# The last chunk of a chunked state scan on three engines, and LayerNorm statistics in quarters

## What is computed

```python
xn = layernorm(x)
s = gated_linear_recurrence(rmsnorm(xn)) + xn        # layer 0, width 256
g = silu(top1_mixture_of_experts(xn))                # 4 experts, 256 -> 1024 -> 256
x = x + s * g
xn = layernorm(x)                                    # layer 1
# state space scan: 512 channels, 16 states n, time step l
xc = silu(causal_conv4(x_half)); delta = softplus(dt)
state[n] = exp(delta * A[n]) * state[n] + (delta * xc) * B[l, n]
y = sum over n of state[n] * C[l, n] + D * xc
s = (y * silu(z)) @ W_out.T + b_out
g = silu(xn @ binarized_W.T + bias)
x = x + s * g
```

## Time and profile before

| | |
|---|---|
| median of 3 runs | 1483.12 us (1483.07 to 6704.92) |
| profiled execution | 1484.12 us, of which its span is 1482.3 us |
| TensorE busy, share of the span | 95% |
| VectorE, ScalarE, GpSimd busy | 69%, 60%, 62% |
| last scan ends | 1452.93 us |
| last tile's store is issued | 1473.69 us |

### The profile page before, as it was taken

One profiled execution on the slowest core, in us unless ns is written; L12 is line 12 of the kernel. 1 busy time (PEld: TensorE's weight loads), 2 busy tenths in 40 slices (PEclk: granted clock), 3 DMA queues, 4 the chain that ended last, 5 costly groups with the idle time before them and its releaser, 6 DMA issues.

```text
span 1482.3 us, 24201 instructions
## 1 busy us (share of the span) xinstructions
PE 1405.9 (95%) x9104; PEld 1126.9 (76%) x9104; DVE 1025.2 (69%) x1348; ACT 887.0 (60%) x1457; POOL 926.4 (62%) x472
## 2 busy tenths in 40 slices
PE   4999999999999999779899999999999999999996
PEld 2454469999999998357777878778778778778875
DVE  6555542332333223588898998998998999989985
ACT  3312121111111111389989999899899899899980
POOL 4422211222222222049989989989899899899994
PEclk9999999999999999899999999999999999999998
DMA  9921136666767663111121211201311211212111
GB/s 314 364 82 57 57 112 242 257 255 235 266 239 271 248 252 127 33 58 34 41 71 44 72 57 44 86 34 40 96 33 44 86 44 35 66 45 78 41 54 43
DMA packets 53284, 172.70 MB, mean 117 GB/s; under 512 B 6064, under 2 KB 32304, under 8 KB 48311
## 3 DMA queue, kind: packets, MB, share of 16 engines
q1 hardware_dynamic: 46038, 150.22, 28.7%
q0 software_dynamic: 7136, 21.01, 4.2%
HBM read 141.78 MB, written 31.00 MB: 117 GB/s over the span
## 4 chain that ended last, share of the span: by engine, by line
PE 71%; POOL 8%; DVE 8%; issue 7%; ACT 4%; DMA 1%; SPq 0%; DVEq 0%; POOLq 0%; ACTq 0%
PE bank L1448 17%; PE bank L1394 9%; PE bank L1628 9%; PE bank L1645 8%; PE bank L1461 8%; POOL hst L654 6%; PE bank L1550 3%; PE bank L1520 3%; DVE hst L1300 3%; PE bank L1586 2%; PE bank L1513 2%; PE bank L1558 2%; PE bank L1423 1%; ACT dA L849 1%; PE bank L1531 1%
## 5 line engine op out<-in xcount | busy, mean ns | idle before, releaser
L1300 DVE TENSOR_TENSOR_SCAN hst<-dA,carry,bank 128x512 f32<-128x512 f32 x512 | 632.7, 1269 | 55.2 <-PE bank L1628 51.6
L654 POOL TENSOR_TENSOR hst<-hst,c_bc 128x2048 f32<-128x2048 f32 x127 | 578.5, 4560 | 23.3 <-DVE hst L1300 8.6
L849 ACT ACTIVATE dA<-delta,negA 128x512 f32<-128x512 f32 x512 | 356.6, 711 | 4.3 <-DVE hst L1300 4.2
L1628 PEld LDWEIGHTS bank<-ident,dbuT 128*128 128x128 f32 x2048 | 242.6, 141 | 139.2 <-issue 73.8
L1628 PE MATMUL bank<-ident,dbuT 128*128 128x128 f32 x2048 | 313.1, 276 | 18.0 <-DVE hst L1300 12.3
L1645 PE MATMUL bank<-ident,hst 128*128 128x128 f32 x2032 | 294.4, 274 | 5.0 <-POOL hst L654 5.0
L838 ACT ACTIVATE dbuT<-duT,bT 128x512 f32<-128x512 f32 x382 | 270.7, 709 | 4.0 <-PE bank L1628 4.0
L1448 PEld LDWEIGHTS bank<-f_sb,w_gu 128*128 128x128 f32 x2240 | 255.5, 192 | 2.7 <-ACT f_sb L721 1.0
L1448 PE MATMUL bank<-f_sb,w_gu 128*128 128x128 f32 x2240 | 256.0, 275 | 0.7 <-ACT f_sb L721 0.7
L1645 PEld LDWEIGHTS bank<-ident,hst 128*128 128x128 f32 x2032 | 236.6, 141 | 5.6 <-POOL hst L654 5.5
L590 POOL TENSOR_TENSOR x_sb<-x_sb,neg_half 128x1 f32<-128x1 f32 x35 | 23.1, 659 | 261.4 <-DVE x_sb L1125 261.4
(11 more groups left out here) (203 smaller groups left out, 1711.3 us busy)
## 6 DMA issues: line engine op xcount, KB each, us to landing
w_gu<-in_w_gu SPq DMA_DIRECT2D x35, 2048.0 KB, 7.3
c_bc<-c_rows SPq DMA_DIRECT2D x64, 512.0 KB, 3.7
sorted_x<-sg_a SPq DMA_DIRECT2D x12, 387.0 KB, 10.9
x_sb<-sorted_x SPq DMA_DIRECT2D x35, 129.0 KB, 7.2
x_sb<-in_x SPq DMA_DIRECT2D x8, 512.0 KB, 7.4
w_d<-in_w_d SPq DMA_DIRECT2D x1, 4096.0 KB, 21.3
x_mix<-x_sb SPq DMA_DIRECT2D x1, 4096.0 KB, 32.0
x_mix<-rt SPq DMA_DIRECT2D x8, 512.0 KB, 2.9
```

Of the source, the lines that this page charges most:

```text
L654: pool.tensor_tensor(h[:], h[:], c, ALU.mult).then_inc(hc_ready, 1)
L849: act.activation(dA[:, at % DA_BUFS, :], delta[q % B][:, d, :], ACT.Exp, scale=negA[:, d, n:n + 1]).then_inc(dA_ready, 1)
L1300: v.tensor_tensor_scan(h[:, d, :], dA[:, at % DA_BUFS, :], bank[4 + u % 2][:], carry1[q % B][:, n, d:d + 1], ALU.mult, ALU.add).then_inc(s ...
L1628: ins = pe.transpose(bank[4 + u % 2][:, i * P:(i + 1) * P], dbuT[(DS * q + n) % DBU_BUFS][:, i, d * P:(d + 1) * P], ident[:])
```

## The change

1. Front: `statistics` takes 8 tiles at a time, four times instead of twice; VectorE's order is two chunks' sums, their statistics, the next two chunks' sums, then the first two chunks' scaled tiles, and so on. GpSimd's `k`-th power waits for the `k`-th statistics.
2. Last chunk, spreads: GpSimd makes those of states 6, 7, 11; that of state 10 is ScalarE's (4 more of line 838).
3. Last chunk, sums: TensorE adds states 0 and 1 up to four units later, state 12 three units earlier, and state 13 within units 61 to 63 instead of after the loop.
4. Last chunk, residual of chunk 6: from GpSimd (after states 12 and 13) to VectorE, between the last tiles; SP stores chunk 6 after it.
5. State 15: no multiplication by C on GpSimd and VectorE. TensorE turns the raw state into banks 6, 7, 4, 5 (16 turns, 9 of them ahead of the last scan's end), where tokens lie on partitions; ScalarE scales each bank by a column `c_last` (a small copy by VectorE in chunk 6) into SBUF; VectorE adds it to the sums and then gates. State 14 is added a tile at a time, its first tile ahead of the last four-block turn.
6. The tiles' residual add goes from GpSimd to VectorE, which reads it from `x_ld`, loaded by SP early in chunk 7 instead of at the end.

```diff
--- before.py
+++ after.py
@@ -52,6 +52,8 @@
...
 POOL_SPREADS = (6, 7, 10, 11)
+LAST_SPREADS = (6, 7, 11)
+LAST_SUMS = {0: (14, 15, 16, 16), 1: (17, 18, 19, 19), 12: (57, 58, 59, 60), 13: (61, 62, 63, 63)}
@@ -95,6 +97,11 @@
...
+SUMS_LAST = [[entry for entry in SUMS_AT[u] if entry[0] or entry[1] not in LAST_SUMS] for u in range(UNITS)]
+for n, at in LAST_SUMS.items():
+    for d in range(DB):
+        SUMS_LAST[at[d]].append((0, n, d))
@@ -107,6 +114,7 @@
...
 FIRST_PIECES = 2
+LAST_TURNED = (6, 7, 4, 5)
@@ -117,6 +125,10 @@
...
     return [name for name in CLAIMS if needs.get(name.rstrip("0123"), needs.get(name[0], turn < CHUNKS - 1))]
+def pool_spreads(q):
+    return POOL_SPREADS if q + 1 < CHUNKS else LAST_SPREADS
@@ -239,6 +251,7 @@
...
         x1 = sb(l1, "x1", [P, TPC, D])
+        c_last = sb(l1, "c_last", [P, TPC])
@@ -500,12 +517,15 @@
...
                         load_x1(q - 1)
+                    if m == 1 and q == CHUNKS - 1:
+                        wait_full(sp, CHUNKS - 3, "XN1")
+                        sp.dma_start(x_ld[:], x1_xn_t[:, tiles_of(q), 0:D]).then_inc(x1_last, 16)
...
                         store_c(q + 1)
-            store_chunk(CHUNKS - 2)
-            load_x1(CHUNKS - 1)
+            sp.wait_ge(res_last, 2)
+            sp.dma_start(out[:, tiles_of(CHUNKS - 2), :], g_out[(CHUNKS - 2) % B][:]).then_inc(stored, 16)
@@ -557,7 +577,7 @@
...
                 part = slice(k * quarter, (k + 1) * quarter)
-                pool.wait_ge(stats_ready, k // 2 + 1)
+                pool.wait_ge(stats_ready, k + 1)
@@ -631,18 +651,11 @@
...
                 make_du(-1, d)
-            def last_state(h):
-                for d in range(DB // 2):
-                    pool.wait_ge(scan_done, unit(CHUNKS - 1, DB * (DS - 1) + d + 1))
-                    pool.wait_ge(c_loaded[1], 64 * CHUNKS)
-                    pool.tensor_tensor(h[:, d, :], h[:, d, :], c_bc[:, STATE_BUFS - 1, :], ALU.mult).then_inc(part_pool, 1)
...
                     if g == CHUNKS * DS - 1:
-                        last_state(h)
@@ -655,15 +668,10 @@
...
                             make_du(q, d)
-                    if n + SPREAD_LEAD in POOL_SPREADS:
+                    if n + SPREAD_LEAD in pool_spreads(q):
                         spread_du(q, n + SPREAD_LEAD)
-                    if q >= 1 and n in POOL_RES:
+                    if 1 <= q < CHUNKS - 1 and n in POOL_RES:
                         residual(q - 1, POOL_RES.index(n))
-            for i in range(TPC):
-                o_st = g_out[(CHUNKS - 1) % B][:, i, :]
-                pool.wait_ge(tile_gated, i + 1)
-                pool.wait_ge(x1_in, 16 * CHUNKS)
-                pool.tensor_tensor(o_st, o_st, x1[:, i, :], ALU.add).then_inc(tile_done, 1)
@@ -827,7 +835,7 @@
...
                 n, i = divmod(p, TPC)
-                if n in POOL_SPREADS:
+                if n in pool_spreads(q):
@@ -899,6 +907,11 @@
...
                     slot(q, u)
+            act.wait_ge(c_turned, 1)
+            for i in range(TPC):
+                act.wait_ge(h_turned, i + 1)
+                act.activation(zy[(CHUNKS - 2) % B][:, i, :], bank[LAST_TURNED[i]][:], ACT.Copy,
+                               scale=c_last[:, i:i + 1]).then_inc(h_scaled, 1)
@@ -925,9 +938,9 @@
...
-                lo = i * TILES // 2
-                part = slice(lo, lo + TILES // 2)
-                v.wait_ge(tile_stats, lo + TILES // 2)
+                lo = i * TILES // 4
+                part = slice(lo, lo + TILES // 4)
+                v.wait_ge(tile_stats, lo + TILES // 4)
@@ -947,21 +960,27 @@
...
-            half = CHUNKS // 2
-            for c in range(half):
-                tile_sums(c)
+            def two_sums(i):
+                tile_sums(2 * i)
+                tile_sums(2 * i + 1)
+            def two_scaled(i):
+                v.wait_ge(rr_ready, i + 1)
+                scaled_tiles(2 * i, 0)
+                scaled_tiles(2 * i + 1, 1)
+            two_sums(0)
             statistics(0)
-            tile_sums(half)
-            v.wait_ge(rr_ready, 1)
-            for c in range(2):
-                scaled_tiles(c, c)
-            for c in range(half + 1, CHUNKS):
-                tile_sums(c)
+            two_sums(1)
+            two_scaled(0)
             statistics(1)
-            for c in range(2, CHUNKS):
-                if c % 2 == 0:
-                    v.wait_ge(rr_ready, c // 2 + 1)
-                scaled_tiles(c, c % 2)
+            two_sums(2)
+            two_scaled(1)
+            statistics(2)
+            two_sums(3)
+            two_scaled(2)
+            statistics(3)
+            two_scaled(3)
@@ -1213,6 +1232,8 @@
...
                 rows = place(t, "BT")[:].rearrange("p (t n) -> p t n", n=P)
+                if t == CHUNKS - 2:
+                    v.tensor_copy(c_last[:], rows[:, :, P - 1]).then_inc(c_turned, 1)
@@ -1300,26 +1321,38 @@
...
                     slot(q, u)
-            last = hst[(DS - 1) % STATE_BUFS]
-            for d in range(DB // 2, DB):
-                v.wait_ge(scan_done, unit(CHUNKS - 1, DB * (DS - 1) + d + 1))
-                v.wait_ge(c_loaded[1], 64 * CHUNKS)
-                v.tensor_tensor(last[:, d, :], last[:, d, :], c_bc[:, STATE_BUFS - 1, :], ALU.mult).then_inc(part_dve, 1)
+            def sum_tile(i):
+                z, h = zy[(CHUNKS - 1) % B][:, i, :], bank[LAST_TURNED[i]]
+                v.wait_ge(h_scaled, i + 1)
+                v.wait_ge(y_tile, i + 1)
+                v.tensor_tensor(h[:], bank[i][:], zy[(CHUNKS - 2) % B][:, i, :], ALU.add).then_inc(y_summed, 1)
+                v.wait_ge(y_summed, i + 1)
+                v.tensor_tensor(z, h[:], z, ALU.mult).then_inc(y_gated, 1)
+            def residual(h):
+                o_st = g_out[(CHUNKS - 2) % B][:, 2 * h:2 * h + 2, :]
+                wait_freed(v, CHUNKS - 1, f"OUT{h}")
+                v.wait_ge(x1_in, 16 * (CHUNKS - 1))
+                v.tensor_tensor(o_st, o_st, x1[:, 2 * h:2 * h + 2, :], ALU.add).then_inc(res_last, 1)
...
                 v.wait_ge(tile_out, i + 1)
-                wait_freed(v, CHUNKS - 1, "G1")
-                v.tensor_tensor(g, bank[TPC + i][:, 0:D], g, ALU.mult).then_inc(tile_gated, 1)
+                v.tensor_tensor(g, bank[LAST_TURNED[i]][:, 0:D], g, ALU.mult).then_inc(tile_gated, 1)
+                v.wait_ge(tile_gated, i + 1)
+                v.tensor_tensor(g, g, x_ld[:, i, :], ALU.add).then_inc(tile_done, 1)
+            v.wait_ge(z_ready, CHUNKS)
+            v.wait_ge(hc_ready, CHUNKS * DS - 1)
             for i in range(TPC):
-                v.wait_ge(y_tile, i + 1)
-                v.wait_ge(z_ready, CHUNKS)
-                z = zy[(CHUNKS - 1) % B][:, i, :]
-                v.tensor_tensor(z, bank[i][:], z, ALU.mult).then_inc(y_gated, 1)
-                if i >= 2:
-                    tile_result(i - 2)
-            for i in range(2, TPC):
+                sum_tile(i)
+            residual(0)
+            wait_freed(v, CHUNKS - 1, "G1")
+            v.wait_ge(x1_last, 16)
+            tile_result(0)
+            residual(1)
+            for i in range(1, TPC):
@@ -1616,10 +1649,11 @@
...
                 n, d = divmod(u, DB)
-                if d == 0 and n in POOL_SPREADS:
-                    pe.wait_ge(dbuT_pool, len(POOL_SPREADS) * q + POOL_SPREADS.index(n) + 1)
+                on_pool = pool_spreads(q)
+                if d == 0 and n in on_pool:
+                    pe.wait_ge(dbuT_pool, len(POOL_SPREADS) * q + on_pool.index(n) + 1)
                 elif d == 0:
-                    made = sum(k not in POOL_SPREADS for k in range(n + 1))
+                    made = sum(k not in on_pool for k in range(n + 1))
@@ -1687,28 +1721,39 @@
...
                         add_skip(q, PE_SKIP.index(u))
-                    for back, n, d in SUMS_AT[u]:
+                    for back, n, d in (SUMS_AT if q + 1 < CHUNKS else SUMS_LAST)[u]:
...
                     slot(q, u)
-            for n in range(DS - 3, DS - 1):
+            def turn_last(i, d):
+                last = hst[(DS - 1) % STATE_BUFS]
+                return pe.transpose(bank[LAST_TURNED[i]][:, d * P:(d + 1) * P], last[:, d, i * P:(i + 1) * P], ident[:])
+            def add_tile(n, i):
+                pe.wait_ge(hc_ready, DS * (CHUNKS - 1) + n + 1)
                 for d in range(DB):
-                    add_up(CHUNKS - 1, n, d)
-            def add_last(d, i):
-                last = hst[(DS - 1) % STATE_BUFS]
-                return pe.matmul(bank[i][:, d * P:(d + 1) * P], last[:, d, i * P:(i + 1) * P], ident[:],
-                                 is_transpose=True, start=False, stop=(d == DB - 1))
+                    ins = pe.matmul(bank[i][:, d * P:(d + 1) * P], hst[n % STATE_BUFS][:, d, i * P:(i + 1) * P],
+                                    ident[:], is_transpose=True, start=False, stop=(d == DB - 1))
+                ins.then_inc(y_tile, 1)
+            for number in (BANK_A, BANK_B):
+                pe.wait_ge(freed[number], count[number])
```

(27 more changed lines are left out.)

8 lines of the change are left out of this document (6 added, 2 removed).

## The result

| | before | changed |
|---|---|---|
| median | 1483.17 us (4 runs, 1483.07 to 6704.92) | 1465.41 us (4 runs, 1465.03 to 1466.01) |
| profiled execution | 1484.12 us, span 1482.3 us | 1466.01 us, span 1464.2 us |

One of the four runs of before took 6704.92 us; the other three lie between 1483.07 and 1483.23. The ratio is 0.9881, 95% interval 0.9861 to 0.99: 17.8 us less, 1.2%. That is within the two per cent to which the prediction gave 0.97. The two executions that were profiled differ by 18.1 us in their spans, and these can be followed from event to event.

A forecast was written before the change was run, and what follows sets the result against it. TensorE was taken as the bound for 71% of the chain, with gains possible only at the two ends. Tail 8.7 plus front 2.1 less 0.2 gave 10.6 us: median 1472.5 us, range 1469.5 to 1477.

The forecast's parts named there:

- the last one of the tail: End of the last tile: last result takes 0.42, 0.04 and 0.42, store at 1465.0 instead of 1473.69, 8.7 us earlier.
- chunk 7's 6.0 us: Last chunk: GpSimd's unbroken run loses one spread and two residuals, so state 14 ends at 1450.75, 6.0 us less.
- Front: Start of the kernel: earlier scaling starts the routing chain 4.4 us earlier; 2.1 us remain at the ranks.
- The stretch of the chain: VectorE's routing chain beside GpSimd's bias splitting: starts at 43.7, ranks at 49.9; 2.3 of the 4.4 us lost.
- 989 behind the next product: Routing chain on VectorE: step 989 waits for GpSimd's next splitting product and ends at 47.2.
- the front keeps its 4.4: Rival, routing chain: splitting leaves the chain alone, all 4.4 us arrive, 1470.2 us; chance 0.12.
- the rival without any gain: Rival, front: chain waits out the whole splitting or TensorE's clock falls, 1474.2 to 1475.2 us, both 1476.9; chance 0.22.
- ScalarE's spreads: Chunk 7: four more spreads cost ScalarE 2.4 us beside 1.64 us of idle time; effect nothing, or 0.8 at worst.
- less in chunk 7: Rival: ScalarE's spreads and waits stop scans, or the first tile takes longer; 3 us less, 1475.5 us; chance 0.19.
- Tail: After state 14 at 1450.8: first projection at 1455.6 instead of 1464.00, 8.4 us earlier; last store 8.7 us earlier.
- VectorE's double steps: Tail: VectorE adds, waits and gates each tile in 2 x 0.72 us, so gated tiles follow each other by 1.44.
- The rival on the other side: Whole kernel slower: `c_last` moves later tiles by 16 bytes; state products 2% slower cost 11 us, at 3% 1490; chance 0.02.

The follow-up runs named there:

- Experiment 1: Changed kernel, with GpSimd also waiting for the last tile and then setting one column of a constant as its last instruction; 1471.6 us.
- experiment 2: Kernel before, with only the last four tiles' residual additions moved from GpSimd to VectorE; 1475.52 us.
- experiment 3: Kernel before, with only the changed kernel's front (statistics in quarters); 1479.42 us.
- experiment 9: Changed kernel, with GpSimd waiting for the one-hot result before it splits the biases, so behind the routing chain; 1466.92 us.
- experiment 11: Changed kernel, with chunk 6's residual added by GpSimd in two halves inside the last chunk, as before, not by VectorE; 1468.09 us.
- experiment 5: Changed kernel, with GpSimd's two rounds of bias splitting put behind the second and third power; 1468.88 us.
- experiment 12: Changed kernel, biases loaded at the start, their splitting spread before the first power, behind the output weights' splitting and behind the one-hot result; 1464.22 us.
- experiment 6: Changed kernel, with state 10's spread back on GpSimd in the last chunk; 1468.63 us.
- experiment 7: Changed kernel, with the spreads of both states 10 and 11 on ScalarE in the last chunk; 1465.55 us.
- experiment 8: Changed kernel, with the last chunk's sums of states 0 and 1 where they were before; 1465.41 us.
- experiment 10: Changed kernel, with state 11's spread on ScalarE and state 10's on GpSimd in the last chunk; 1465.54 us.
- experiment 4: Changed kernel, with the front of the kernel before; 1467.44 us.

## Why the prediction was wrong, and where it was right

**The failed step is the last one of the tail.** "The last result is 0.42, 0.04 and 0.42: store at 1465.0, not 1473.69, 8.7 us earlier" was taken for the gain of the whole execution. So the 8.61 us between the last store's issue and the end of the span were carried over as if they belonged to the store. They belonged to GpSimd. The change takes GpSimd's last instruction from 1473.66 to 1447.65, and in the prediction that counted only as chunk 7's 6.0 us. The rows of line 132 stood in the trace of before: SyncE done at 1475.6, the end at 1482.3, GpSimd's drain between. Experiment 1 puts it back for 6.2 us of the median; experiment 2 takes it away from before for 7.4, of which some 0.3 are the shorter addition (0.42 us on VectorE, 0.72 on GpSimd) and the rest, 7.1, lies within what its executions differ from 6.5. With the 6.5 us the forecast would have been 1466.0, 0.6 above the measured median. None of the rivals had this place either.

**Front: right in mechanism, 0.9 us short in size.** Scaled tiles at 11.96 (forecast 11.6), the first turn at 13.47 (13.1), both 0.4 late because chunk 2's load came 0.48 later than in the profile of before; the second pair at 19.95 (19.8), the chain's start at 43.81 (43.7). The stretch of the chain was forecast as 6.2 us long and was 5.28: ranks at 49.09, not 49.9. The step of the list that failed is "989 behind the next product": line 1008, its counterpart, took 0.28 and waited for nothing, apparently since it started in the very moment in which GpSimd's product did (both 45.58; 45.03 and 45.04 in experiment 3, where it took 0.28 as well), and so the products of 45.58 and 47.25 held 1010 and 1012, where the list had them hold 989 and 991 and a cast 993. The steps before it came as forecast: 1005 over at 44.78 (44.8), 1007 at 45.65 (988 at 45.7). The rival "the front keeps its 4.4" fell by these two rows, the rival without any gain by the ranks at 49.09 and by a granted clock of 1.00 from 43 to 52 us: TensorE idled 1.79 us before the ranks, not 2.7. Whether 2.7 would have been harmless, as the forecast took it from one wait of 2.53 us, was therefore never put to the test; experiments 9 and 11 have waits of 2.53 us after which the clock was at the lower level, so that one row was no ground to go by. Experiments 5, 9 and 12 show the cause by taking it away three times: 3.33 us each time from the chain's start to the ranks.

**The Trainium skill** (SBUF — State Buffer, Who interferes with whom) gives a wider rule than the prediction used. It names, besides instructions with two SBUF inputs, also `tensor_scalar` and casts in their two-port modes as ones that can contend for the port that VectorE shares with GpSimd. This case's rows agree in what was held: the scaling of experiment 5 took 3.90 instead of 1.37 beside GpSimd's products, while the sums over tiles, for which it names no conflict, took 2.78 beside the same work in experiment 12, and 2.71 alone. Whether the scaling ran in such a mode is not shown, and its time speaks against it: alone it took 0.41 us for 256 columns, as much as a sum over 256 columns (0.41), while a `tensor_scalar` elsewhere in the changed kernel (line 1156) did 512 columns in 0.43. Other rows speak for a limit to it: in the changed kernel the eight tiles scaled at 30.89 and 32.19 took 1.38 for four, as they do alone, beside GpSimd's power of 5.43 us from 30.82, so a GpSimd instruction that computes long on few elements held nothing that could be seen.

**Chunk 7: right.** GpSimd unbroken, its run 5.92 us shorter (forecast 6.0). ScalarE's spreads cost one wait of 1.1 us for the scans (forecast 0 to 0.8), and it did not reach the end, for TensorE's last early turn and GpSimd's state 14 end within 0.01 us of each other (1447.66, 1447.65). That neither clock alone would give more is what experiments 6, 7 and 11 found: a spread more on GpSimd 3.2 us, two residuals 2.7, a spread less nothing. The rival "less in chunk 7" has no time here.

**Tail: right.** From the end of state 14 to the first projection the sum gave 4.85 us, measured were 5.00 (7.23 before). The first projection comes 11.35 - 3.20 = 8.15 us earlier apart from what the front gives, forecast 8.4; the last result 11.60 - 3.20 = 8.4, forecast 8.7. VectorE's double steps follow each other by 1.33 (forecast 1.44), and the granted clock stayed at 1.00 from 1444 to 1460 us, while in before it was 0.63 from 1456 to 1460.

**The rival on the other side** (slower, by tiles moved 16 bytes) fell: GpSimd's state products take 4.557 us in the mean, 4.56 before.

The sum of measured terms, in the profiled pair: 3.20 (front, as it arrives at chunk 7) + 5.92 + 2.48 + 6.5 = 18.1. The first of them is the least certain. State 2's product in chunk 7 began between 1376.27 and 1378.23 in the eight profiles that share the new front and the middle (the changed kernel and experiments 1, 3, 6, 7, 8, 10 and 11), and between 1379.42 and 1381.43 in the three with the old front (before, experiments 2 and 4), so up to 2 us of any such number may be the execution's own. The means of the two groups are 1377.35 and 1380.29, 2.9 apart, which fits the 2.96 us at the ranks; experiment 3's median says 3.5. By luck the changed kernel's profile was the latest of its group and before's the latest of the other, so that 3.20 came out near the mean. Where within the 1300 us between these 2 us arise was not followed.

## What to carry to other kernels

Ask of the last microseconds, in which nothing computes, to whom they belong: look at each engine's closing rows and not only at the last store, and let the engine with the long closing work end early. Before moving GpSimd's work into idle time, go through all that VectorE does beside it, scalings, casts and scans too, not only through the chain that is to be freed. And when two engines meet at a bound, an experiment on either side of the meeting point (one operation more, one less) tells whether anything is left there.

## What the runs showed of the hardware

- GpSimd's closing drain ended 8.4 to 8.5 us after its last instruction in all 14 profiles, whether that was an addition, a product, or a memset of one column (before 1473.66 to 1482.1; changed 1447.65 to 1456.1; experiment 1 1461.81 to 1470.2; experiment 2 1457.21 to 1465.7). VectorE's took 0.46 us, ScalarE's 0.61, TensorE's 2.9 to 3.0.
- A VectorE instruction held by GpSimd was over 0.15 to 0.16 us after the GpSimd instruction that held it (lines 1005, 1007, 1010 and 1012). The four scans of 0.23 us each took up to 1.68 each beside the splitting (experiment 9).
- The idle time just before does not alone decide what TensorE's clock does. In experiment 5 it was idle for 3.38 us before 21.75, and its next eight turns took 1.09 with a granted clock of 1.00 (21 to 24 us); it was idle for 2.70 us before 30.86, and they took 1.97 with 0.56. In between it had worked for 6.4 us, before the first of the two for 5.6. A wait of 2.53 us stands in three kernels: before 24.52 in before, followed by 1.00; before 56.30 in experiment 9 and before 1449.16 in experiment 11, followed by 0.52 both times. Why one and the same wait was followed by either level was not tested.
